# A transformer block on one core: two vector-side waits on GpSimd's last addition of each half tile

## The reference, cut to what matters

```python
def attn_layer(x, Wqkv, qs, ksc, Wo):        # x is shift_tokens(x)
    qkv = x @ Wqkv
    q, k, v = jnp.split(qkv, 3, -1)
    q = l2norm(q) * qs
    k = l2norm(k) * ksc
    q = q * cos * scale + rotate_half(q) * sin * scale
    k = k * cos * inv + rotate_half(k) * sin * inv
    out = local_attention(q, k, v)           # windows of 32, softmax over 64 keys
    return out @ Wo
```

## Time and profile before

| what | us |
|---|---|
| median of 3 runs | 4038.45 |
| the profiled execution, its own time | 4040.95 |
| its span, first to last instruction | 4038.8 |
| PE busy | 3574.6 (89%) |
| DVE busy | 3179.5 (79%) |
| ACT busy | 3017.5 (75%) |
| POOL busy | 2501.3 (62%) |

### The profile page before, as it was taken

The page is one execution under the profiler, slowest core; times in us unless marked ns, Lnnn a source line. Parts: engine busy times, 40 slices in busy tenths (PEclk is TensorE's granted clock), DMA queues, the critical chain, the costliest instruction groups (busy, mean ns, idle before and its releaser), DMA issues.

```text
span 4038.8 us, 94411 instructions
## 1 busy us (share of the span) xinstructions
PE 3574.6 (89%) x30888; PEld 2698.8 (67%) x30894; DVE 3179.5 (79%) x4346; ACT 3017.5 (75%) x6096; POOL 2501.3 (62%) x2313
## 2 busy tenths in 40 slices
PE   5898689999889999789999799999799999799998
PEld 3444367777567777577776577776577776577776
DVE  5665488886788886788986788886788886889876
ACT  3556488886688887688886688886688886688885
POOL 3554377774477773577773677773677773677762
PEclk8999799999999999999999899999899999899999
DMA  4222100000000001000001000001000001000002
GB/s 129 87 88 92 45 2 0 0 0 14 16 1 0 0 0 28 1 1 0 0 0 28 1 1 0 0 0 28 2 1 0 0 0 28 2 1 0 0 1 69
DMA packets 59720, 67.55 MB, mean 17 GB/s; under 512 B 12006, under 2 KB 40164, under 8 KB 58468
## 3 DMA queue, kind: packets, MB, share of 16 engines
q1 hardware_dynamic: 59492, 64.64, 5.5%
HBM read 46.27 MB, written 18.35 MB: 16 GB/s over the span
## 4 chain that ended last, share of the span: by engine, by line
issue 43%; POOL 33%; PE 15%; ACT 5%; DVE 2%; DMA 1%; POOLq 1%; SPq 0%; ACTq 0%; DVEq 0%
POOL sb_area L1522 14%; PE bank L401 12%; POOL sb_area L1508 9%; POOL sb_area L1530 6%; PE bank L614 2%; POOL sb_ptT L1548 2%; ACT sb_area L790 2%; ACT sb_area L983 1%; DVE sb_area L1157 1%; ACT sb_area L940 1%; POOL sb_xwin L1548 1%; DMA sb_wqk_lo<-qk_rows 1%; ACT sb_lnb L952 1%; ACT sb_area L842 0%; ACT sb_lnb L949 0%
## 5 line engine op out<-in xcount | busy, mean ns | idle before, releaser
L790 ACT ACTIVATE sb_area<-bank 128x512 f32<-128x512 f32 (+4 forms) x2149 | 1336.7, 649 | 444.2 <-PE bank L614 381.0
L1508 POOL TENSOR_TENSOR sb_area<-sb_area 128x512 f32<-128x512 f32 x768 | 994.1, 1294 | 829.2 <-DVE sb_area L1259 828.2
L1259 DVE TENSOR_TENSOR sb_area<-bank,sb_rots 128x1024 f32<-128x1024 f32 x768 | 905.2, 1217 | 325.8 <-ACT sb_area L940 323.5
L401 PE MATMUL bank<-sb_area 128*64 128x64 f32 (+6 forms) x17104 | 1048.5, 275 | 11.3 <-DMA sb_area<-in_c_crot 3.6
L401 PEld LDWEIGHTS bank<-sb_area 128*64 128x64 f32 (+4 forms) x17104 | 747.8, 146 | 279.8 <-issue 237.6
L1522 POOL TENSOR_TENSOR sb_area<-sb_area,sb_rn 128x512 f32<-128x512 f32 x768 | 785.0, 1044 | 15.8 <-ACT sb_rn L956 15.4
L614 PE MATMUL bank<-sb_ident,sb_area 128*128 128x128 f32 x3072 | 493.5, 284 | 289.3 <-POOL sb_area L1522 152.5
L401 PE MATMUL bank<-sb_area,sb_wvo 128*128 128x256 f32 x3072 | 728.4, 381 | 3.1 <-DVE sb_xT L1314 3.1
L401 PE MATMUL bank<-sb_wqk_hi,sb_xwin 128*128 128x512 f32 x1536 | 606.2, 436 | 54.5 <-DVE sb_xwin L1239 48.7
L614 PEld LDWEIGHTS bank<-sb_ident,sb_area 128*128 128x128 f32 x3072 | 340.7, 142 | 440.5 <-POOL sb_area L1522 224.5
L401 PEld LDWEIGHTS bank<-sb_area,sb_wvo 128*128 128x128 f32 x3072 | 556.0, 191 | 74.3 <-issue 8.8
(11 more groups left out here) (115 smaller groups left out, 4300.5 us busy)
## 6 DMA issues: line engine op xcount, KB each, us to landing
qk_rows<-sb_p SPq DMA_DIRECT2D x52, 256.0 KB, 4.1
sb_wqk_hi<-qk_rows SPq DMA_DIRECT2D x32, 256.0 KB, 2.9
sb_wqk_lo<-qk_rows SPq DMA_DIRECT2D x32, 256.0 KB, 2.7
sb_area<-in_Wqkv SPq DMA_DIRECT2D x7, 1024.0 KB, 5.9
sb_area<-in_WvT SPq DMA_DIRECT2D x7, 512.0 KB, 7.4
sb_wo_bd<-in_Wo SPq DMA_DIRECT2D x14, 256.0 KB, 8.4
sb_area<-in_x SPq DMA_DIRECT2D x4, 512.0 KB, 6.2
sb_area<-in_x SPq DMA_DIRECT2D x8, 256.0 KB, 2.9
```

The lines of the kernel that those rows point to most:

```text
L401: return nc.tensor.matmul(o, a, b, start=start, stop=stop, skip_group_check=True)
L790: return nc.scalar.activation(o, i, ACT.Copy)
L1259: tt_(t12[:, c % 2, :, :].rearrange("p u (h d) -> p u h d", h=8), src, bc(rots[:, tt, s, :, :], [P, 2, 8, D], 2), ALU.mult).then_inc(S["ro ...
L1508: pt_(qn[:, c, :].rearrange("p (h e d) -> p h e d", h=8, e=2), t12[:, c % 2, 0, :].rearrange("p (h e d) -> p h e d", h=8, e=2), swapped, A ...
```

## The change

Before the two token copies of `load_next`, DVE waits until GpSimd has done addition 3 of the newest tile, and before `rests_of_tile` until it has done addition 1. With `(tt, bt)` the tile that is loaded (two ahead) or split (one ahead), the two values are one more than the number of additions up to there. The loads and splits ahead of the pipeline, and the first step's skipped split, are as before.

```diff
                     def load_next():
                         if v := behind(t, i, part, -2):
+                            tt, bt = v
+                            dve.wait_ge(S["add"], (g_of(bt) * 4 + tt) * 4 - 3)
                             load_tile(*v, not (part == 0 and t + 2 < TT))
...
                         if wp == 0:
                             update()
                             if not (part == 0 and t == 0) and (v := behind(t, i, part, -1)):
+                                tt, bt = v
+                                dve.wait_ge(S["add"], (g_of(bt) * 4 + tt) * 4 - 1)
                                 rests_of_tile(*v)
                         else:
                             load_next()
```

## The result

The changed kernel took 4049.51 us (median of 20 runs) against 4042.93 for the kernel before beside it; the ratio is 1.0016 with a 95% interval of 1.0010 to 1.0023, which is 6.5 us (4.0 to 9.3). The forecast was +4 us. The time itself, 4049.51 us, is 7 us above the 4042.5 of the forecast, and 4.5 of these 7 us are the kernel before, which took 4042.93 beside it and not 4038.45. The profiled execution has a span of 4043.5 us, 4.7 more than before.

A forecast was written before the change was run, and what follows sets the result against it. PE and ACT were taken to bound the steady tiles, which pay nothing; the layer starts pay 3 x 1.0 + 3 x 0.4 = 4.2 us, rounded to 4, giving 4038.45 + 4 = 4042.5 us, range 4034 to 4053.

The forecast's parts named there:

- What bounds the kernel: Steady tiles: PE and ACT form the ring, DVE has over a microsecond to spare; layer starts are a separate case.
- The steady tiles at nothing: Steady tiles: the waits cost nothing, hidden by DVE's idle time until ACT's square; uncovered, 0.2 to 0.5 us a tile.
- The slide of half 1: Steady tile, after the rest: later work starts 0.2 us late, 0.3 with a register operation more, 0.5 in one of four.
- The slack left: Steady tile, ahead of the next rotation 0: 0.3 to 0.5 us of DVE's 1.19 us of idle time remains.
- Rival 1: Steady tiles, copies at the end of half 1: the cover runs out, slower, 4051 to 4095 us; chance 0.23.
- The release: Between a wait's end and its instruction: 0.05 to 0.1 us, register operations at the copies adding up to 0.25.
- The starts at 4.2 us: First tiles of six layers: three layers pay 1.0 us each, three at a low clock 0.4 each.
- The copies of tile 0: First tile of a layer: copies waiting for addition 3 delay the next rotation by 0.1 us.
- the copies of tiles 1 and 2: Second and third tiles of a layer: waiting copies add 0.1 us, then 0.1 to 0.3 us.
- the rest in tile 1: Second tile of a layer: the rest waiting for addition 1 makes the rotation behind it 0.5 us late.
- Rival 2: GpSimd's additions, no longer held up, set the pace: 13 us faster, 4025 us; chance 0.10.

The follow-up runs named there:

- e8: Changed kernel plus a VectorE reduction of 768 elements between the wait and the copies, everywhere but in a layer's first six steps; 1.0077 to the kernel before.
- e12: Changed kernel plus a 128x512 memset between the wait and the rest, everywhere but in a layer's first six steps; 1.0026 to the kernel before.
- e2: Kernel before plus only the wait for addition 3, ahead of the copies; 1.0010 to the kernel before.
- e11: Changed kernel plus a 128x512 memset between the wait and the rest, in a layer's first six steps only; 1.0041 to the kernel before.
- e1: Kernel before plus only the wait for addition 1, ahead of the rest, first timing; 0.9987 to the kernel before.
- e9: Kernel before plus only the wait for addition 1, ahead of the rest, timed again; 0.9996 to the kernel before.
- e4: Changed kernel with both waits everywhere but in a layer's first six steps; 1.0005 to the kernel before.
- e6: The changed kernel once more, unaltered; 1.0009 to the kernel before.
- e7: Changed kernel plus a 128x512 memset between the wait and the copies, in a layer's first six steps only; 1.0027 to the kernel before.
- e10: Kernel before with the two token copies moved to GpSimd behind its addition 3, as additions of zero; 1.0008 to the kernel before.

## Why the prediction was right

**What bounds the kernel** held. Steady stretches are 2139.3 to 2140.0 us with the waits or without, while DVE gives up 222 us of its 323.5 us of idle time ahead of the rotations. One sentence there was too narrow: PE's transposes behind GpSimd's scalings are not the one path on which lateness of DVE and POOL comes back. In e8 and e12 it came back through ACT's mask copy, which waited 226.1 and 238.9 us for DVE's subtraction.

**The steady tiles at nothing** held, by the mechanism given. The slide of half 1 was put at 0.2 to 0.3 us; from rotation 0 to rotation 2 of the tile it is 1472.86 - 1465.71 = 7.15 us, against 1471.18 - 1464.28 = 6.90 before. The two rotations 0, before and after, are

```profile
1464.28 2.36 DVE L1259 TENSOR_TENSOR sb_area<-bank,sb_rots 128x1024 f32<-128x1024 f32 x2 [1.31 <-ACT sb_area L940]
```

```profile
1465.71 2.36 DVE L1261 TENSOR_TENSOR sb_area<-bank,sb_rots 128x1024 f32<-128x1024 f32 x2 [0.53 <-ACT sb_area L940]
```

The slack left was put at 0.3 to 0.5 us, and 0.29 to 0.53 is what the rows show. Rival 1 was near: it needed 0.3 to 0.5 us more than the waits cost, and e12 with 0.45 us more pays its first 0.06 us a tile. The interval of the time, 4.0 to 9.3 us, leaves the low end of that rival, some +12 us with the starts, not far outside; the steady stretches, which don't grow, are what rules it out.

**The release** was put at 0.05 to 0.1 us, plus up to 0.25 where register operations stand behind the wait. It is 0.12 at the rest, with one of them, and 0.32 at the copies in the loop, with three; it is 0.03 at the copies of a layer's first tile, where the trace has none.

**The starts at 4.2 us** came out near as a sum (3.4 from the means, with an error of 1.5), with its terms mis-sized, so that the nearness is in part luck. At a like clock a layer pays 0.5 us where I had 1.0 and 0.15 where I had 0.4. The copies of tile 0, +0.1, are +0.18 in the mean; I had counted 0.06 us of overlap between the second copy and the rotation, and the rotation starts 0.03 us after the copies end. I had put +0.1 and +0.1 to 0.3 on the copies of tiles 1 and 2. The third step is 0.24 longer in the mean, but at a like clock it is 0.15, and not from the copies alone: e2 has 13.58 us there like before, and a dose at the rest reaches it in full (e11). The largest term, +0.5 for the rest in tile 1, is there and not in the sum: with that wait alone (e1, e9) three layers take 12.31 or 12.32 us in the second step for 11.83 or 11.84 in one layer each of before and e4, and then 13.11 or 13.12 in the third for 13.98. The granted clock of that third step was 1.00 in the three layers and 0.88 in the other two, so the shorter step goes with a clock that didn't fall there. Whether the later work brought that about, the runs don't show.

**The timed ratio** of 6.5 us (4.0 to 9.3), and 3.6 us in e6 (-0.4 to 8.1), overlap with the 3.6 us of the traces (about 0.6 to 6.5). Whether the rest of the first figure, 3 us, is chance or a larger share of layers at a low clock stays open: the second step was over 14.3 us in 11 of the 30 layers whose copies don't wait and in 12 of the 24 whose copies do (16 of 36 with e8 and e12), which is too near to tell, though the doses of e7 and e11 made that share larger.

**Rival 2**, GpSimd's gain, had all that it asked for: no addition over 1.307 us, 8.4 us less busy time on L1512. It brought nothing, since the additions wait for rotations 839 us, and e10 shows the same without any wait on VectorE. The rule of the Trainium skill, page "SBUF — State Buffer", section "Who interferes with whom" (whoever comes first keeps the pair for the whole instruction, and the other one blocks), agrees with both traces: copies and rests of 1.1 to 1.4 us have become 0.22 and 0.29 where no addition runs beside them.

## What to carry to other kernels

A wait that keeps two engines from colliding doesn't save the time of the collision if one of them is only held up behind the other: it moves the same time ahead of the instruction and adds the release. Cost such a wait at both ends of a loop, for in this pipeline 1.29 us lay between the end of the addition and the next rotation in a steady tile, and 0.36 us in the first tile of a layer, six times over. And where a start-up varies with the clock, compare steps over many layers and executions: one pair of spans showed 4.7 us here, of which 2.7 lay in work that had not been changed.

## What the runs showed of the hardware

- In one execution of the kernel before, the granted clock of the second tile of a layer was 0.65 to 0.92, and the stretch from its rotation 0 to the next one took 14.47 us in the layer at 0.65 and 11.83 in the one at 0.92.
- After a wait for another engine, VectorE's instruction started 0.03 us after the end of GpSimd's addition with no register operation between, 0.12 with one and 0.32 with three.
- A two-input VectorE operation of 128x128 elements took 0.28 us beside an addition that it was ahead of, and 1.42 us beside one that had started 0.01 us earlier; it ended 0.15 us after that addition.
- On GpSimd an addition of a zero column to 64x128 elements takes 0.39 us, VectorE's copy of them 0.21.
